# A recurrent two-layer kernel on one core: half-width unpacking of 4-bit weights, and the last rows' normalization placed later

## What is computed

```python
xn = _layernorm(x)
s = _L0_attn_ref(xn, ...)           # 16 heads, gated delta-rule recurrence, then @ Wo
g = _silu(_L0_ffn_ref(xn, ...))     # 512 -> 1408 -> 512, silu gate
x = x + s * g
xn = _layernorm(x)
s = _L1_attn_ref(xn, ...)           # block-diagonal gates, h = a * h + x
g = _silu(_L1_ffn_ref(xn, ...))     # 512 -> 4096 -> 512, gelu gate, 4-bit weights
x = x + s * g
...
def dequant_nvfp4(W_packed, scales, block=32):   # two 4-bit codes in each int
    low, high = W_packed & 15, W_packed >> 4 & 15
    vals = NVFP4_LUT[interleave(low, high)]      # 0 .5 1 1.5 2 3 4 6 and negatives
    return vals * scales                         # one scale per 32 values
```

## Time and profile before

| | |
|---|---|
| median of 3 runs | 3052.25 us (3050.41 to 3053.97) |
| the profiled execution's own time | 3056.1 us |
| its span in the profile | 3054.3 us |
| TensorE busy | 2968.3 us (97% of the span) |
| VectorE, ScalarE, GpSimd busy | 2068.2, 1816.4, 1764.2 us |
| mean granted TensorE clock | 0.989 of full speed |

### The profile page before, as it was taken

One profiled execution on the slowest core, in us unless ns is written; L12 is line 12 of the kernel. 1 busy time (PEld: TensorE's weight loads), 2 busy tenths in 40 slices (PEclk: granted clock), 3 DMA queues, 4 the chain that ended last, 5 costly groups with the idle time before them and its releaser, 6 DMA issues. The chain is left out here.

```text
span 3054.3 us, 62437 instructions
## 1 busy us (share of the span) xinstructions
PE 2968.3 (97%) x23512; PEld 2448.2 (80%) x23512; DVE 2068.2 (68%) x3545; ACT 1816.4 (59%) x4333; POOL 1764.2 (58%) x2620
## 2 busy tenths in 40 slices
PE   8999988999999999999999979989999999999998
PEld 7878776888888888888888868778888888888887
DVE  6899976778788788888788733454455556455445
ACT  5312146878778877788878753355545555455553
POOL 2233225767666666676676644645566676566555
PEclk9999999999999999999999989999999999999999
DMA  3465541121111111111112035521112244121112
GB/s 109 150 188 169 184 141 35 50 52 57 57 49 49 48 57 54 43 50 50 57 57 57 30 119 180 165 93 52 59 59 63 64 148 140 49 63 59 53 49 103
DMA packets 164556, 252.80 MB, mean 83 GB/s; under 512 B 13520, under 2 KB 89040, under 8 KB 164224
## 3 DMA queue, kind: packets, MB, share of 16 engines
q1 hardware_dynamic: 151824, 231.54, 24.8%
q10 hardware_dynamic: 12368, 17.04, 1.6%
q0 software_dynamic: 64, 0.23, 0.0%
HBM read 185.58 MB, written 63.18 MB: 81 GB/s over the span
## 5 line engine op out<-in xcount | busy, mean ns | idle before, releaser
L77 PE MATMUL bank<-b_XH,b_wh 128*128 128x512 f32 x1152 | 508.7, 442 | 14.0 <-ACT b_zt L1285 10.3
L1536 DVE SCALAR_TENSOR_TENSOR b_zt<-b_rx,b_cw,b_zt 128x512 f32<-128x512 f32 x576 | 470.7, 817 | 23.8 <-POOL b_rx L1745 3.1
L79 PE MATMUL bank<-b_XH,b_wl 128*128 128x512 f32 x1152 | 455.7, 396 | 0.0
L78 PE MATMUL bank<-b_XL,b_wh 128*128 128x512 f32 x1152 | 453.9, 394 | 0.0
L2998 DVE TENSOR_TENSOR b_QACC<-b_QACC,bank 128x512 f32<-128x512 f32 x240 | 164.6, 686 | 306.4 <-PE bank L79 306.3
L1791 POOL TENSOR_TENSOR b_PR<-b_A,b_T 128x15 f32<-128x15 f32 (+7 forms) x480 | 168.8, 352 | 173.3 <-issue 138.4
L77 PEld LDWEIGHTS bank<-b_XH,b_wh 128*128 128x128 f32 x1152 | 219.3, 190 | 49.3 <-ACT b_zt L1285 12.3
L79 PEld LDWEIGHTS bank<-b_XH,b_wl 128*128 128x128 f32 x1152 | 217.8, 189 | 49.8
L2463 POOL TENSOR_TENSOR b_wl<-b_wS,b_wh 128x512 fp32r<-128x512 f32 x128 | 181.2, 1417 | 108.9 <-ACT b_wh L2457 108.5
L78 PEld LDWEIGHTS bank<-b_XL,b_wh 128*128 128x128 f32 x1152 | 220.4, 191 | 25.0
L3093 POOL TENSOR_TENSOR b_HL<-b_g,b_HH 128x512 fp32r<-128x512 f32 x128 | 186.4, 1456 | 87.6 <-ACT b_HH L2843 87.6
(11 more groups left out here) (301 smaller groups left out, 8741.6 us busy)
## 6 DMA issues: line engine op xcount, KB each, us to landing
b_abc<-tmp_a SPq DMA_DIRECT2D x64, 256.0 KB, 3.6
...
```

The source lines that it names most:

```text
L77: e.do.matmul(out, wh, xh, start=first and k == 0, stop=False)
L78: e.do.matmul(out, wh, xl, start=False, stop=False)
L79: m = e.do.matmul(out, wl, xh, start=False, stop=last and k == n - 1)
L1536: e.do.scalar_tensor_tensor(out=z[:, :], in0=rx[:, j:j + 512], scalar=cw[:, u // 2, KIND[name[0]], j:j + 1], in1=z[:, :], op0=ALU.mult, op ...
```

## The change

It has three parts.

**Unpacking.** The 512 code words of a tile (two codes each in the low byte of an int32) are first joined in pairs to 256 words of four codes, and spread so that each byte holds one code as an 8-bit float (e5m2); the two scaling instructions read single bytes with a step of four. Codes stay in `b_pk`; the tile `b_wq` is written only by the scaling. The semaphore `dq` counts 8 per tile.

```diff
-    a, b = w[:, 1, :].bitcast(I32), w[:, 0, :].bitcast(I32)
-    e.wait_ge("tb", 3)
-    e.wait_ge(f"kq{s % 2}", 16 * (s // 2))
-    e.do.tensor_scalar(b, pk, 0xF0, 12, bitwise_and, logical_shift_left)
-    e.do.scalar_tensor_tensor(a, pk, 15, b, bitwise_and, bitwise_or)
-    e.do.tensor_scalar(b, a, 9, 0x0E000E00, logical_shift_left, bitwise_and)
-    e.do.tensor_scalar(a, a, 12, -0x7FFF8000, logical_shift_left, bitwise_and)
-    e.do.tensor_tensor(a, a, b, bitwise_or)
+    a, b = pk[:, 0:256], pk[:, 256:512]
+    e.do.tensor_scalar(pk, pk, 0xFF, 1, bitwise_and, logical_shift_left)
+    e.do.scalar_tensor_tensor(a, b, 16, a, logical_shift_left, bitwise_or)
+    e.do.tensor_scalar(b, a, 0x01E001E0, 4, bitwise_and, logical_shift_left)
+    e.do.scalar_tensor_tensor(a, a, 0x001E001E, b, bitwise_and, bitwise_or)
+    e.do.tensor_scalar(b, a, 3, -0x7F7F7F80, logical_shift_left, bitwise_and)
+    e.do.scalar_tensor_tensor(a, a, 0x0E0E0E0E, b, bitwise_and, bitwise_or)
...
 def weight_scaled(e, t, s):
+    e.wait_ge("tb", 3)
+    e.wait_ge(f"kq{s % 2}", 16 * (s // 2))
+    e.wait_ge("dq", 8 * s + 6)
     for s2 in range(2):
-        e.wait_ge("dq", 7 * s + 5 + s2)
-        e.do.scalar_tensor_tensor(w[:, s2, :], half[:, :, s2], 16384.0, sc, mult, mult)
+        e.do.scalar_tensor_tensor(w[:, s2, :], <bytes s2, s2 + 4, ...>, 16384.0, sc, mult, mult)
```

**First operands of the second feed-forward part** (mix0):

```diff
-            if n == 3 and c in (6, 7, 8, 9):
-                first_block_high(e, ft, c - 6)
+            if n == 3 and c in (4, 5, 7, 8):
+                first_block_high(e, ft, (4, 5, 7, 8).index(c))
...
-            if n == 3 and c == 3:
-                first_blocks_dve(e, ft)
-            if n == 3 and c == 10:
-                for x in range(4):
-                    first_block_low(e, ft, x)
-            if n == 3 and c == 11:
-                weight_sums(e, ft, 0)
+            if n == 3 and c in (2, 3, 4, 5):
+                first_block_dve(e, ft, c - 2)
+            if n == 3 and c in (6, 7, 8, 9):
+                first_block_low(e, ft, c - 6)
+            if n == 3 and c in (10, 11, 12):
+                weight_sums(e, ft, 0, c - 10)
...
-        if i in (50, 51, 52, 53):
-            first_block_pool(e, ft, i - 50)
+        if i in (34, 37):
+            first_block_pool(e, ft, 1 if i == 34 else 3)
+        if i in (48, 49):
+            first_block_pool(e, ft, 2 * (i - 48))
```

**Row tiles 12 to 15** (ffn1): the fills, and DVE's and ACT's parts of the normalization, which leave the fills for places of their own; the first three rate steps; one wait of DVE's adds.

```diff
-RATE_AT = {4: 0, 10: 1, 16: 2, 22: 3, 40: 4, 46: 5, 52: 6, 58: 7}
+RATE_AT = {5: 0, 11: 1, 17: 2, 22: 3, 40: 4, 46: 5, 52: 6, 58: 7}
...
     if g == 0:
-        at[2] += [("sum", 12, 0), ("sum", 13, 0)]
+        at[3] += [("sum", 12, 0), ("sum", 13, 0)]
     if g == 1:
-        at[0] += [("sum", 14, 0), ("sum", 15, 0)]
-        at[2] += [("turn", 12, 0), ("turn", 13, 0)]
+        at[0] += [("sum", 14, 0)]
+        at[3] += [("sum", 15, 0)]
     if g == 2:
-        at[0] += [("turn", 14, 0), ("turn", 15, 0)]
+        at[0] += [("turn", 12, 0), ("turn", 13, 0)]
+    if g == 3:
+        at[1] = [("turn", 14, 0), ("turn", 15, 0)] + at[1]
...
+        if g in (1, 2):                       # ACT, ahead of gelu0(g)
+            norm_root_act(e, m, 10 + 2 * g)
+            norm_root_act(e, m, 11 + 2 * g)
...
+        if g == 1:                            # DVE, ahead of hidden0(0)
+            norm_stats_dve(e, m, 12)
+            norm_stats_dve(e, m, 13)
...
+        if g == 1:                            # DVE, behind hidden1(0)
+            norm_stats_dve(e, m, 14)
+        if g in (1, 2):
+            norm_dve(e, m, 10 + 2 * g)
+            norm_dve(e, m, 11 + 2 * g)
...
             e.wait_ge("row1", 16)
-            e.wait_ge("yt", 16)
             e.wait_ge("wo", 64)
+            if o == 3:
+                e.wait_ge("yt", 16)
```

More of the change, by code:

```diff
@@ L9 @@
 F32R = mybir.dt.float32r
-F16 = mybir.dt.float16
+F8 = mybir.dt.float8e5
 I32 = mybir.dt.int32
@@ L858, in head_high @@
     elif s < 5:
-        e.wait_ge("dq", 7 * 48)
+        e.wait_ge("dq", 8 * 48)
     else:
@@ L2266, in ffn1_tiles @@
     t.puts("HL", [128, 512], F32R, [o + 2048 for o in hidden])
-    t.puts("QACC", [128, 1024], F32, [arena + o for o in (53504, 57600, 61696, 67584)])
+    t.puts("QACC", [128, 1024], F32, [arena + o for o in (53504, 57600, 67584, 61696)])
     for i, n in enumerate(("l1x", "l1y", "l1m")):
@@ L2294, in first_block_pool, with first_block_dve @@
 def first_block_pool(e, t, x):
-    e.wait_ge("yl", 8)
-    hi, lo = block(t, ("b12", "b11", "b22", "b21")[x])
+    b = ("b12", "b11", "b22", "b21")[x]
+    e.wait_ge("yl", 4 if b[2] == "1" else 8)
+    hi, lo = block(t, b)
     to = first_form(t, ("t3", "t1", "t2", "t4")[x])
     e.do.tensor_tensor(to, f32(hi), f32(lo), ALU.add).then_inc(e.sems["bf"], 1)
-def first_blocks_dve(e, t):
+def first_block_dve(e, t, x):
     t1, t3, t2, t4 = (first_form(t, n) for n in FIRST_BLOCKS)
     bt = e.sems["bt"]
[L2306 to L2314, removed]
+    e.wait_ge("bf", (3, 4, 4, 4)[x])
+    if x == 0:
+        e.do.tensor_tensor(t1, t3, t1, ALU.subtract).then_inc(bt, 1)
+    if x == 1:
+        e.wait_ge("bt", 1)
+        e.do.tensor_tensor(t3, t2, t3, ALU.subtract).then_inc(bt, 1)
+    if x == 2:
+        e.wait_ge("bt", 2)
+        e.do.tensor_tensor(t2, t2, t1, ALU.subtract).then_inc(bt, 1)
+    if x == 3:
+        e.wait_ge("bt", 3)
+        e.do.tensor_tensor(t4, t4, t2, ALU.subtract).then_inc(bt, 1)
 def first_block_high(e, t, x):
@@ L2337, in weight_fetch @@
     pk, sc = t["pk"][s % 2], t["sc"][s % 2]
[L2338 removed]
+    e.wait_ge("dq", 8 * (s - 2) + 8)
     n = {"G": "gate", "U": "up", "D": "down"}[p]
@@ L2391, in weight_codes @@
 def weight_codes(e, t, s):
-    n, w, pk, dq = 7 * s, t["wq"][s % 2], t["pk"][s % 2], e.sems["dq"]
-    a, b = w[:, 1, :].bitcast(I32), w[:, 0, :].bitcast(I32)
+    n, pk, dq = 8 * s, t["pk"][s % 2], e.sems["dq"]
+    a, b = pk[:, 0:256], pk[:, 256:512]
+    e.wait_ge(f"pk{s % 2}", 32 * (s // 2 + 1))
+    e.do.tensor_scalar(pk[:, :], pk[:, :], 0xFF, 1, ALU.bitwise_and, ALU.logical_shift_left).then_inc(dq, 1)
+    e.wait_ge("dq", n + 1)
+    e.do.scalar_tensor_tensor(out=a, in0=b, scalar=16, in1=a, op0=ALU.logical_shift_left, op1=ALU.bitwise_or).then_inc(dq, 1)
@@ new lines, in weight_codes @@
+    e.wait_ge("dq", n + 2)
+    e.do.tensor_scalar(b, a, 0x01E001E0, 4, ALU.bitwise_and, ALU.logical_shift_left).then_inc(dq, 1)
+    e.wait_ge("dq", n + 3)
+    e.do.scalar_tensor_tensor(out=a, in0=a, scalar=0x001E001E, in1=b, op0=ALU.bitwise_and, op1=ALU.bitwise_or).then_inc(dq, 1)
+    e.wait_ge("dq", n + 4)
+    e.do.tensor_scalar(b, a, 3, -0x7F7F7F80, ALU.logical_shift_left, ALU.bitwise_and).then_inc(dq, 1)
+    e.wait_ge("dq", n + 5)
+    e.do.scalar_tensor_tensor(out=a, in0=a, scalar=0x0E0E0E0E, in1=b, op0=ALU.bitwise_and, op1=ALU.bitwise_or).then_inc(dq, 1)
@@ L2395, in weight_codes, with weight_scaled @@
+def weight_scaled(e, t, s):
+    w = t["wq"][s % 2]
+    codes = t["pk"][s % 2][:, 0:256].bitcast(F8).rearrange("p (n k) -> p n k", k=4)
     e.wait_ge("tb", 3)
     e.wait_ge(f"kq{s % 2}", 16 * (s // 2))
[L2397 to L2411, removed]
     e.wait_ge(f"sc{s % 2}", 32 * (s // 2 + 1))
+    e.wait_ge("dq", 8 * s + 6)
@@ L2413, in weight_scaled @@
     for s2 in range(2):
-        e.wait_ge("dq", 7 * s + 5 + s2)
-        e.do.scalar_tensor_tensor(out=w[:, s2, :], in0=half[:, :, s2], scalar=16384.0, in1=t["sc"][s % 2][:, :],
+        at = bass.AP(tensor=codes.tensor, offset=codes.offset + s2, ap=[list(codes.ap[0]), [2, 2], [4, 256]])
+        e.do.scalar_tensor_tensor(out=w[:, s2, :].rearrange("p (h n) -> p h n", h=2), in0=at, scalar=16384.0,
+                                  in1=t["sc"][s % 2][:, :].rearrange("p (h n) -> p h n", h=2),
                                   op0=ALU.mult, op1=ALU.mult).then_inc(e.sems["dq"], 1)
@@ L3032, in fill @@
                 row(what[1])
-            if what[0] == "sum" and what[1] % 2:
-                for i in (what[1] - 1, what[1]):
-                    norm_stats_dve(e, m, i)
-                for i in (what[1] - 1, what[1]):
-                    norm_dve(e, m, i)
     for g in range(2 * STEPS + 4):
@@ L3047, in ffn1_dve @@
             weight_sums(e, t, j + 1, 0)
+        if g == 1:
+            norm_stats_dve(e, m, 12)
+            norm_stats_dve(e, m, 13)
+        if g == 2:
+            norm_stats_dve(e, m, 15)
         if older:
```

5 lines of the change are left out of this document (1 added, 4 removed).

## The result

The changed kernel takes 3034.47 us (median of 4 runs, 3034.31 to 3039.18), the kernel before 3052.54 in the same comparison: ratio 0.994, 95% interval 0.9928 to 0.9952, or 18.1 us less.

The account below looks back on a forecast made before the run. TensorE, busy 97% of the span, was taken as the bound, so only its waits and clock count. 3056.1 - 6.2 (front) - 8.5 (start of ffn1 with mix0) = 3041.4 profiled, less 3.85 gives 3037.5; range 3025 to 3046.

Parts of the forecast that it names:

- The front: First feed-forward part: faster unpacking shortens PE's three waits for `b_ACC`, 14.7 us in all, by 6.2 us.
- mix0: Stage before ffn1: sums moved into earlier idle time bring ffn1's first product to 2003.85, a net gain of 1.6 us.
- the start of ffn1: Beginning of the second feed-forward part: later row work shortens PE's waits; -8.5 us together with mix0.
- The tile: DVE's unpacking of one tile with POOL idle: 3.76 us instead of 4.11; beside POOL 0.27 us less per tile.
- The slower rival: Unpacking: bytes read with a step cost DVE more, deciding from scalings of 1.15 us; 3069 at 1.38; chance 0.06.
- What reaches PE: Front: nine of 32 tiles have late codes and save nothing; 23 tiles at 0.27 us shorten waits by 6.2 us.
- the waits left, about 3.5, 2.5 and 2.5 us, still cost the clock in this reckoning: Front: PE's three shortened waits for `b_ACC` still lower its granted clock, so no clock gain is counted.
- the clock is kept as well: Rival for the front: waits shrink to about 2 us and keep full clock; 3030.5, or 3021.4 without waits; chance 0.18.
- The "2 us" for `b_mol`: mix0: two `b_TF` sums behind products 48 and 49 make product 50 come about 2 us late.
- The wait of 2.9 us for `gelu0(1)`: Start of ffn1: PE idles 2.9 us before `m1(2)` until ACT finishes this gelu at 2025.8.
- That of 1.0 for the mixing: Start of ffn1: PE waits 1.0 us for DVE's mixing, ending at 2011.7, instead of 2.24.
- Rates and `b_QACC`: Second feed-forward part: later rate steps and the moved accumulator cost nothing, hidden by PE's products.

Follow-up runs that it names:

- experiment 1: The kernel before with the new unpacking alone, mix0 and the second feed-forward part as before: 3042.13 us, ratio 0.9966.
- Experiments 7: The changed kernel with SyncE's code-word transfers ahead of the finished tile's store and the scales' behind it: 3028.81 us, ratio 0.9919.
- 12: The kernel before, old unpacking, with SyncE's code-word transfers ahead of the store and the scales' behind it: 3048.66 us, ratio 0.9987.
- 3: The kernel before with the moves inside mix0 alone; fills, rates and unpacking as before: 3049.21 us, ratio 0.999.
- experiment 4: The kernel before with only three rate steps one step later, two accumulator tiles exchanged and one wait moved: 3053.53 us, ratio 1.0002.
- kernel 2: The changed kernel with the unpacking of before, so only the rows', mix0 and rate moves: 3043.54 us, ratio 0.9968.
- Experiment 9: The changed kernel with ACT's roots of row tiles 12 to 15 behind gelu0 and DVE's normalizations behind third_sum: 3032.51 us, ratio 0.9931.

## Why the prediction was right, and where its terms were off

The forecast of 3037.5 us stands 3.0 above the median and inside its own range. Its mechanisms were right: DVE's shorter tiles reach PE through the waits for `b_ACC`, and the rows' work placed later takes PE's waits at the start of ffn1. That the sum came so near is in part luck. The front gave more than its term, since less clock was lost; so did mix0; and the start of ffn1 gave no more than its term, probably less. A few sums slip by up to 0.2 us without changing the forecast's sense: the mixing ended 7.84 us behind 2005.44 (not 7.7), ACT's list adds up to 2025.6 (not 2025.8), and the upper bound for a tile is 0.63 (not 0.61).

- **The tile.** 3.80 us against my 3.76; half-width instructions of 0.43 and 0.29, the pair's gain 0.12; scalings from bytes 0.69 us in experiment 1's and the changed kernel's rows (709 ns mean with POOL's stretches). The slower rival, with its 1.15 us and more, is refuted. In the step with POOL the gain is 0.23 instead of 0.27.
- **What reaches PE.** I let nine of 32 tiles give nothing, since their codes came late. The two profiles differ by 7.7 us of waits; the means of the profiles in the table of the experiments' section differ by 7.1, from 13.8 to 6.7. With 0.22 us a tile (the median step is 5.52 against 5.74), 32 tiles would make 7.0 and 23 of them 5.1, so all tiles seem to count; with sums that differ by up to 3.7 us under the same front this isn't shown. The waits for codes are as uncertain, 11.3 to 15.1 us with the old unpacking and 8.7 to 18.1 with the new. Experiments 7 and 12 show that the fetch was a price of its own, some 4 us with the old unpacking and 8 with the new.
- **The clock in the front.** The step that failed is "the waits left, about 3.5, 2.5 and 2.5 us, still cost the clock in this reckoning". They were 3.5, 1.9 and 1.6 and cost 3.4 us where before's cost 8.1. The mean over the profiles in that table is 2.3 us with the new unpacking and 6.8 with the old. This is the rival "the clock is kept as well", in part, and with it the front gives -10.9 by experiment 1 (interval -6.4 to -14.0), not -6.2. Some 2 us of it went into the fourth wait for `b_zt`.
- **mix0.** -3.0 us by the traces and -3.8 by the times (interval -0.3 to -5.8), not -1.6. The "2 us" for `b_mol` near product 50 came as a wait of 1.3 us. The idle time up to ffn1 fell from 3.4 to 1.6 us; the other 1.2 us I can't place.
- **Start of ffn1.** The wait of 2.9 us for `gelu0(1)` came, 2.83 us long. That of 1.0 for the mixing didn't. From first product to `m1(2)` it is 21.4 us, forecast 22.05. But the 31.0 us that I set against it held 3.1 us of lost clock, and kernels 1, 3 and 4 pass the old part in 28.4, 28.6 and 27.4. By the medians the rows' part is worth 9.5 - 3.8 = 5.7 us (some 4 either way) where my sum had 6.9. The two profiles say 8.0 from the first product to 2400 us, but kernels 1, 3 and 4, with the old part, lead the profile of before by 2.6, 3.9 and 4.7 there; against them it is 3.3 to 5.4 (and 4.6 to 6.7 by kernel 2's 9.3). So this term was, if anything, too large.
- **Rates and `b_QACC`.** Nothing that could be told from noise, as costed (experiment 4).

By the table of the Trainium skill, "VectorE: DVE Perf Modes", section on the TRN2 errata, my estimate was 0.47 us less for the six code instructions. They took 2.58 us, from 218.55 to 221.13, against 2.77, so 0.19 less, and the row decides.

The Trainium skill, "ScalarE: Activation LUTs", section "Rules for kernel authors", advises doing all functions of one table set before switching. Experiment 9 loads tables as often as the changed kernel (51 times in either trace), and only moves the roots' loads behind the gelu that PE waits for, which took the wait of 2.83 us away.
